# Four heads' negated maxima as twelve shared rows, and another table of preparation tasks

## What is computed

```python
Q = proj(query, wq_w, wq_b)
K = proj(key, wk_w, wk_b)
V = proj(value, wv_w, wv_b)
scale = 1.0 / np.sqrt(HEAD_DIM).astype(np.float32)
scores = jnp.einsum('bhqd,bhkd->bhqk', Q, K) * scale
causal = jnp.tril(jnp.ones((S, S), dtype=bool))
scores = jnp.where(causal, scores, -jnp.inf)
attn = jax.nn.softmax(scores, axis=-1)
out = jnp.einsum('bhqk,bhkd->bhqd', attn, V)
out = out.transpose(0, 2, 1, 3).reshape(B, S, D_MODEL)
return out @ wo_w.T + wo_b
```

## Time and profile before

| | us |
|---|---|
| median of 3 runs | 721.07 |
| lowest, highest | 720.25, 721.08 |
| the profiled execution's own time | 726.71 |
| its span, first to last instruction | 724.5 |
| PE busy | 581.1 (80%) |
| DVE busy | 363.0 (50%) |
| ACT busy | 278.2 (38%) |
| POOL busy | 196.8 (27%) |
| mean granted TensorE clock | 0.919 |

### The profile page before, as it was taken

The page is one execution under the profiler, slowest core; times in us unless marked ns, Lnnn a source line. Parts: engine busy times, 40 slices in busy tenths (PEclk is TensorE's granted clock), DMA queues, the critical chain, the costliest instruction groups (busy, mean ns, idle before and its releaser), DMA issues.

```text
span 724.5 us, 11632 instructions
## 1 busy us (share of the span) xinstructions
PE 581.1 (80%) x3942; PEld 339.5 (47%) x3942; DVE 363.0 (50%) x791; ACT 278.2 (38%) x458; POOL 196.8 (27%) x253
## 2 busy tenths in 40 slices
PE   3799999999988888999999998520199999999800
PEld 2557667574744445555455553310044555455400
DVE  4573535143175655775687573269433333333535
ACT  3132241414045555666665666100033333332204
POOL 2251403140221131123123123100234444433315
PEclk9999999999979999999999998855599999999955
DMA  7794000010422322152233551067079999997564
GB/s 232 253 379 144 2 0 0 0 59 32 142 77 102 112 77 90 66 177 78 72 114 129 161 169 68 0 232 301 23 269 386 399 397 403 392 407 222 137 216 146
DMA packets 41141, 120.68 MB, mean 167 GB/s; under 512 B 3680, under 2 KB 25872, under 8 KB 38032
## 3 DMA queue, kind: packets, MB, share of 16 engines
q1 hardware_dynamic: 35792, 113.44, 42.5%
q0 software_dynamic: 4608, 6.29, 4.3%
q10 hardware_dynamic: 704, 0.47, 0.3%
HBM read 96.07 MB, written 22.02 MB: 163 GB/s over the span
## 4 chain that ended last, share of the span: by engine, by line
PE 58%; DMA 14%; DVE 13%; issue 5%; SPq 4%; ACT 4%; POOL 1%; ACTq 0%; DVEq 0%; POOLq 0%
PE PS L1783 9%; PE PS L1493 8%; PE PS L1502 8%; DMA sums<-row 4%; SPq L545 4%; DMA arena<-ctx_in 4%; PE PS L1646 3%; PE PS L1577 3%; PE PS L1659 3%; PE PS L1815 3%; PE PS L1618 3%; PE PS L1796 2%; PE PS L1464 2%; PE PS L1569 2%; PE PS L1481 2%
## 5 line engine op out<-in xcount | busy, mean ns | idle before, releaser
L1004 DVE TENSOR_REDUCE Mx<-PS 128x1 f32<-128x384 f32 (+3 forms) x176 | 103.0, 635 | 55.4 <-PE PS L1618 55.0
L1338 ACT ACTIVATE arena<-PS 128x512 f32<-128x512 f32 (+1 forms) x176 | 90.8, 559 | 46.0 <-PE PS L1646 44.7
L731 POOL TENSOR_SCALAR_AFFINE_SELECT arena<-arena 128x512 f32<-128x512 f32 x64 | 40.8, 637 | 181.8 <-ACT arena L1338 181.7
L1646 PE MATMUL PS<-arena 99*128 99x512 bf16 (+3 forms) x256 | 63.3, 310 | 11.0 <-ACT arena L1338 8.9
L1618 PE MATMUL PS<-arena 96*128 96x128 bf16 (+3 forms) x256 | 64.2, 310 | 0.0
L1493 PE MATMUL PS<-arena 128*128 128x512 f32 x128 | 56.1, 593 | 3.2 <-ACT arena L1253 1.6
L1502 PE MATMUL PS<-arena 128*128 128x256 f32 x256 | 55.9, 379 | 0.0
L1174 DVE TENSOR_TENSOR X<-PS,Y 128x512 f32<-128x512 f32 x48 | 31.0, 687 | 46.3 <-PE PS L1796 46.2
L1410 ACT ACTIVATE X<-X 128x512 f32<-128x512 f32 x48 | 29.4, 630 | 63.1 <-DVE X L1174 63.0
L1502 PEld LDWEIGHTS PS<-arena 128*128 128x128 f32 x256 | 48.6, 190 | 6.6
L1659 PE MATMUL PS<-arena 128*32 128x128 f32 (+3 forms) x512 | 48.5, 449 | 1.1 <-POOL arena L731 1.0
(11 more groups left out here) (191 smaller groups left out, 973.4 us busy)
## 6 DMA issues: line engine op xcount, KB each, us to landing
ring_a<-experts SPq DMA_DIRECT2D x12, 2048.0 KB, 14.5
arena<-experts SPq DMA_DIRECT2D x12, 2048.0 KB, 15.1
ring_a<-experts SPq DMA_DIRECT2D x12, 512.0 KB, 10.6
sums<-zrow SPq DMA_DIRECT2D x3, 2048.0 KB, 20.3
arena<-pieces SPq DMA_DIRECT2D x32, 192.0 KB
arena<-experts SPq DMA_DIRECT2D x12, 512.0 KB, 13.4
arena<-pieces SPq DMA_DIRECT2D x32, 128.0 KB
pieces<-arena SPq DMA_DIRECT2D x4, 768.0 KB, 3.7
```

Source lines behind the costliest of these rows:

```text
L731: pool.affine_select(out=pb[j % 2][:, :, 0:P], in_=pb[j % 2][:, :, 0:P], compare_op=ALU.is_ge, fill=0.0, base=0, pattern=[[0, GH], [1, P]] ...
L1004: dve.tensor_reduce(Mx[:, g % 2, i, heads[0]:heads[-1] + 1], bank(score_banks[(g * NSH + u) % 3])[:, 0:len(heads) * w] .rearrange("p (h n) ...
L1338: act.activation(pb[j % 2][:, heads[0]:heads[-1] + 1, 0:w], bank(exp_banks[(g * NSH + n) % 2])[:, 0:len(heads) * w] .rearrange("p (h n) -> ...
L1646: mm = pe.matmul(bank(exp_banks[(g * NSH + n) % 2])[:, a * w:(a + 1) * w], KTs[0:SX, g * GH + h, j * P:(j + 1) * P], QTs[0:SX, g * GH + h, ...
```

## The change

`minus_max` turns all four heads of a tile at once: 4 transposes of 12 columns (4 heads times 3 pieces) instead of 16 of 3 columns. The result stands once, as 12 rows, and ACT copies it under each head; it still makes two copies of 1024 columns, now of 12 rows. So that each head takes only its own three rows of the twelve, the keys' rows hold ones in the three rows of that head and zeros in the other nine. This pattern is summed from the identity by one small DVE instruction (`own`), and POOL copies it instead of setting ones. The contraction grows from 99 to 108 rows. `minus_max` now uses spare bank 5 alone.

The table `TASKS` is another one. Most of its tasks now stand in the first list, within the shifted scores, and few share a slot. Both value projections of a batch are now made in the batch before, so that of the first batch stands wholly ahead of the slots. In the third tile's slot the cut of the first scores moves from (3, 4) to (2, 3): the last bank of scores comes after `values`.

```diff
-SX = SK + NPC
+SX = SK + GH * NPC
...
-CUTS = [(3, 3), (4, 4), (3, 4), (0, 0)]
+CUTS = [(3, 3), (4, 4), (2, 3), (0, 0)]
...
 TASKS = {
...
-    (1, 0): ([], [], [], [("split_q", 0, 1)]),
-    (1, 1): ([("key", 0, 1)], [], [("key", 1, 1)], []),
...
+    (0, 1): ([("key", 0, 1)], [], [], []),
...
+    (1, 3): ([("output", 1, -1)], [], [("split_q", 0, 1)], [("stats", 0, -1)]),
...
+        own = sb("own", [P, GH])
...
-        ntp = signal("ntp", NG * 2)
+        ntp = signal("ntp", NG)
...
+            pool.wait_ge(owns, 1)
...
-                pool.memset(KTs[SK:SX, GH * g:GH * g + GH, :], 1.0).then_inc(ones, 1)
+                pool.tensor_copy(KTs[SK:SX, GH * g:GH * g + GH, :],
+                                 own[SK:SX, :].unsqueeze(2).to_broadcast([SX - SK, GH, T]))\
+                    .then_inc(ones, 1)
...
+            dve.tensor_reduce(own[SK:SX, :], ident[SK:SX, SK:SX]
+                              .rearrange("p (h c) -> p h c", h=GH), AX.X, ALU.add)\
+                .then_inc(owns, 1)
...
             def minus_max(b, g):
 
+                act.wait_ge(ntp.s, ntp.now(b, g + 1))
                 for m in range(2):
-                    act.wait_ge(ntp.s, ntp.now(b, 2 * g + m + 1))
                     act.activation(QTs[SK:SX, GH * g + 2 * m:GH * g + 2 * m + 2, :],
-                                   spare(m).bitcast(BF16)[SK:SX, :]
-                                   .rearrange("p (h n) -> p h n", h=2), ACT.Copy)\
+                                   wide(spare(0).bitcast(BF16)[SK:SX, 0:T], 2), ACT.Copy)\
                         .then_inc(nte.s, 1)
...
             def minus_max(b, g):
                 pe.wait_ge(mneg.s, mneg.now(b, 4 * (g + 1)))
-                for m in range(2):
-                    o = take(m, nte, nte.now(b, 2 * g + m + 1)).bitcast(BF16)
-                    for h in range(2):
-                        for i in range(TT):
-                            mm = pe.transpose(o[SK:SX, (TT * h + i) * P:(TT * h + i + 1) * P],
-                                              nst[:, g % 2, i, 2 * m + h, :], identb[:])
-                    mm.then_inc(ntp.s, 1)
+                o = take(0, nte, nte.now(b, 2 * g + 2)).bitcast(BF16)
+                for i in range(TT):
+                    mm = pe.transpose(o[SK:SX, i * P:(i + 1) * P],
+                                      nst[:, g % 2, i].rearrange("p h c -> p (h c)"), identb[:])
+                mm.then_inc(ntp.s, 1)
```

More of the change, by code:

```diff
@@ L75 @@
 TASKS = {
-    (0, 0): ([("value", 1, 0)], [], [], []),
-    (0, 1): ([("query_in", 0, 1)], [], [], [("query_in", 1, 1)]),
-    (0, 2): ([], [], [("heads", 1, -1)], [("query", 0, 1), ("query", 1, 1)]),
-    (1, 0): ([], [], [], [("split_q", 0, 1)]),
-    (1, 1): ([("key", 0, 1)], [], [("key", 1, 1)], []),
-    (1, 2): ([("split_k", 0, 1), ("output", 0, -1)], [], [], []),
-    (1, 3): ([("output", 1, -1)], [], [("stats", 0, -1)], []),
-    (2, 1): ([("norm", 0, -1)], [("value", 0, 1)], [], []),
-    (2, 2): ([], [("turn", 0, -1)], [("turn", 1, -1)], []),
-    (3, 0): ([("heads", 0, 0), ("bias", 0, 0)], [], [], []),
-    (3, 2): ([], [], [("logits", 0, -1)], []),
+    (0, 0): ([("query_in", 0, 1)], [], [], []),
+    (0, 1): ([("key", 0, 1)], [], [], []),
+    (0, 2): ([("query_in", 1, 1)], [], [], []),
+    (0, 3): ([], [], [("key", 1, 1)], [("heads", 1, -1)]),
+    (1, 0): ([("query", 0, 1)], [], [], []),
+    (1, 1): ([("output", 0, -1)], [("split_k", 0, 1), ("query", 1, 1)], [], []),
+    (1, 3): ([("output", 1, -1)], [], [("split_q", 0, 1)], [("stats", 0, -1)]),
+    (2, 0): ([("value", 0, 1)], [], [], []),
+    (2, 2): ([], [], [], [("heads", 0, 0)]),
+    (2, 3): ([], [], [("norm", 0, -1)], []),
+    (3, 0): ([("turn", 0, -1), ("bias", 0, 0)], [], [], []),
+    (3, 1): ([], [], [], [("turn", 1, -1)]),
+    (3, 2): ([("logits", 0, -1)], [], [], []),
+    (3, 3): ([("value", 1, 1)], [], [], []),
 }
@@ L354, in build @@
         ones = sem("ones")
+        owns = sem("owns")
         vpr = signal("vpr", 2)
@@ L1012, in negate @@
                 dve.wait_ge(mxs.s, mxs.now(b, NSH * (g + 1)))
-                dve.wait_ge(ntp.s, ntp.now(b, 2 * (g - 1)) if g >= 2
-                            else ntp.before(b, 2 * (NG + g - 1)))
+                dve.wait_ge(ntp.s, ntp.now(b, g - 1) if g >= 2 else ntp.before(b, NG + g - 1))
                 dve.tensor_scalar(d[:, :, :, 0], m, -1.0, None, ALU.mult).then_inc(mneg.s, 1)
@@ L1748, in _ @@
             with pe.Fori(1, B - 1) as b:
-                read_by.update({m: (nte.s, nte.now(b, m + 1)) for m in range(2)})
+                read_by.update({0: (nte.s, nte.now(b, 2)), 1: (vev.s, vev.now(b, 2))})
                 slots(b, pe_slot)
-            read_by.update({m: (nte.s, nte.now(B - 1, m + 1)) for m in range(2)})
+            read_by.update({0: (nte.s, nte.now(B - 1, 2)), 1: (vev.s, vev.now(B - 1, 2))})
             slots(B - 1, pe_slot, last=True)
```

## The result

| | before | after |
|---|---|---|
| median, us (4 runs each) | 721.08 | 793.3 |
| lowest, highest | 720.25, 722.38 | 789.62, 794.68 |
| the profiled execution's own time | 726.71 | 789.62 |
| its span | 724.5 | 787.1 |
| mean granted clock | 0.919 | 0.882 |

The changed kernel takes 1.096 times as long by all runs, 95% interval 1.091 to 1.101; the quotient of the two medians is 1.100. The page of after: PE's line, its slices, and its granted clock in the same slices.

The account below looks back on a forecast made before the run. PE by busy share, with SP's queue a hidden bound of the same length that the change makes decide. Third batch's first group 453.2 + 335.6 + 0.5 = 789.3 us span, 786 median; forecast 769 to 803, range 762 to 804.

Parts of the forecast that it names:

- six stands: PE in attention: waits for contexts 20, 14 and 15 us, for pieces 8 to 9 us each, together about 74.
- from span to median: Whole kernel: profiled execution lies 5.6 us over the runs' median; the same shift takes 789.3 to 786 us.
- The ring: SP's queue in attention: context, keys, splits, pieces out, reads, next context, 62.9 and 65.4 us round, as long as PE's bound.
- faster rival: Slot (0,1): context in time when PE arrives, PE the bound, gain at most 10.7 us, 710 to 717 us; chance 0.03.
- the short queue: SP's queue drained at context issue: lag from 14.8 towards 4.3 us, 10.5 off each of two loops, 765 us; chance 0.07.
- Landing of context 1: First batch: landing left at 233.1 us, since the queue still had work; without that cover 235.
- From landing to last split: Context landing to the queries' split in (1,3): 26.6 us in the first batch, 29.9 in the others.
- one slow clock: After an idle stretch, before the last split: granted clock 0.72 over 6 us, 1.7 us lost.
- Two writes: SP sends queries' and keys' pieces in a row: 6.4 us, between 4.35 for one and 8.7 for two.
- Reads to the next context: SP's queue, first read of pieces to next context's landing: 49.0 us, 50.3 with the outputs' two writes among them.
- First group in the third batch: Start of reads to the first group's landing, letting slot (3,0) of the third batch go on: 15.2 us.
- The transposes: PE, minus_max: 0.67 us a group saved, 0.4 taken as between; 16 groups at most 10.7 us.

Follow-up runs that it names:

- the early context: Changed kernel with a second context buffer, SP issuing the context of the batch after next ahead of the reads of pieces: 739.2 us, ratio 1.025.
- keys back: Changed kernel with key projections back at (1,1), keys' split, first output projection and second half of queries behind them in (1,2): 751.1 us, ratio 1.041.
- the old turns: Kernel before, with its old transposes, given the new table and cuts, second value projection back from (3,3) to (0,0): 800.4 us, ratio 1.104.
- my own edit: Changed kernel with second context buffer, context issued ahead of the reads, keys split at (1,0), queries at (1,1): 732.2 us, ratio 1.010.

## Why the prediction was right

The sign, the mechanism and the six stands were right, and 793.3 us lies in the range, 7 over the forecast of 786. The sum met the span to 2.2 us, partly by errors that cancel, and the 7 us are the step from span to median. Point by point:

**The ring.** Shown by the early context: moving one transfer ahead of the reads takes away every context wait and 50.8 us of the span. The faster rival (context in time) falls with it, and so does the short queue: the lag of the context stayed 14.6 to 15.4 us, although the reads had been held back.

**The sum's terms,** on the profile's clock. Landing of context 1: 230.8, not 233.1; SP issued it 2.2 us earlier, at 215.41. I had kept the old landing because of a queue that still had work; it moved with the slots. From landing to last split: 28.9, 30.2 and 31.1 us against 26.6, 29.9 and 29.9, 3.7 too little in all. The first batch is the mis-sized one, 2.3 us. I gave one slow clock 1.7 us there, and it cost 2.8; the 3.3 us for the queries' last part were an estimate, and what the other 1.2 us are was not looked into. Two writes: 6.6, 8.0 and 6.1 against 6.4, within the bounds. Reads to the next context: 47.6 and 48.6 against 49.0 and 50.3. First group in the third batch: 13.5 against 15.2. From there to the end: 335.7 against 336.1. The reads of the third batch begin at 437.89 where the sum has 438.0, but only because the errors cancel (-2.3, +3.7, +1.5, -3.1). The span came out 2.2 us under the sum, mostly by the first group.

**The stands.** Predicted 20, 14 and 15 us for contexts, measured 17.0, 15.9 and 15.0 (in the first, PE came at 213.9 us and not at 212.5, and the context 2.3 us earlier than I had it); predicted 8 to 9 for each of the pieces, measured 5.0, 7.9 and 6.2. Together 66.8, not 74.

**From span to median.** This step failed. I took 5.6 us off because the profiled execution of before lay so far above its median; that of after was the lowest of its four, 3.7 below. By the spans the change costs 62.6 us, by the medians 72.2 (65.8 to 72.9 by the ratio's interval). In the later comparisons before alone ran from 719.1 to 729.8 us, so an execution's distance from its median can't be carried over.

**The transposes.** The price of 0.67 us a group on PE was right (11.0 us for 16 groups). That the waits give most of it back I had not named: POOL's select, hidden by the old transposes, is what is late next.

**The cut.** I gave it no term at all. In the changed kernel that is right (791.4 against 793.3); with the old table the same number costs 16.7 us with one context buffer and 18.7 with two, by the medians. The new table hides most of it where a projection stands ahead of the turn. The keys' half does so in (0,3): moved away in keys back, or missing in the last batch, it leaves a wait of 1.8 to 2.0 us where there was 0.3 at most. The value projection does so in (3,3): moved away with the old turns, it leaves 1.8 to 1.95 us where there was none. Neither was moved alone in the changed kernel with all else kept.

**What stays open.** Of the new table's remaining 13 us the stands explain the size, but the bank wait is of my own edit; where a best place of the splits would end was not run. With keys back the span ended 6 us over its expectation, and the wait for the maxima grew by 5.8; that the one is the other fits by size only. What the shared rows alone are worth in the changed kernel was not measured either.

## What to carry to other kernels

Before moving a task that waits for a transfer to an earlier slot, find what lets the transfer start, follow that chain once round, and compare its length with the busy time of the engine that looks like the bound: here both were 63 us, and a projection four slots earlier became a stand of 15 to 17 us a batch. Where the ring binds, the order in one DMA queue is worth a look before the table of tasks: one transfer moved ahead won back 54 us here, the keys moved back 42. Where the engine binds, removing its short instructions pays only as far as nothing stood hidden behind them. Two knobs of a schedule (here the cut and the table) have to be tried together: the cut that cost nothing with one table cost 17 to 19 us with the other.

## What the runs showed of the hardware

A transfer of 512 KB issued behind 24 reads of pieces landed 14.9 us after its issue, and 6.2 us when issued ahead of them. The DMA engines were not full then: behind the context's issue at 298.79 us the share was 0.60 for 4.2 us and 0.12 for the other 11 until it landed. The windows of after, columns as above:

```profile
298.80:303.00 4.20, 0.00 (x0) 0.00 (x0) 0.47 (x2) 0.00 (x0) 0.00 (x0) 0.78 0.60 166
303.00:314.00 11.00, 0.00 (x0) 0.00 (x0) 0.00 (x0) 0.00 (x0) 0.00 (x0) 0.50 0.12 49
```

In the first window 697 KB moved (166 GB/s). If the reads went on at the 49 GB/s of the second, they were about 206 of these, and the other 491, by this estimate, were most of the context's 512 KB. A share of 0.12 is the work of two engines in sixteen, so it looks as if the context's end waited for a few engines on which the reads still stood. That is argued from the rates; which engine moved what no run here shows.

Two writes of 768 KB issued 0.4 us apart let the reads begin 6.1 to 8.0 us after the first issue, so they overlap in part: one alone took 4.35 us, and two in a row without overlap would be 8.7.
